# Two graph attention layers on one core: the products for the last layer's vectors, the columns' matmul and a wait of ScalarE are placed anew

## The reference

```python
def gat_layer(x, W, a_s, a_d, b, edge_index, concat):
    h = (x @ W).reshape(n, H, C)
    alpha_s = jnp.einsum('nhc,hc->nh', h, a_s)
    alpha_d = jnp.einsum('nhc,hc->nh', h, a_d)
    e = jax.nn.leaky_relu(alpha_s[src] + alpha_d[dst], NEG_SLOPE)
    m = jax.ops.segment_max(e, dst, num_segments=n)
    e = jnp.exp(e - m[dst])
    denom = jax.ops.segment_sum(e, dst, num_segments=n)
    alpha = e / (denom[dst] + EPS)
    out = jax.ops.segment_sum(h[src] * alpha[:, :, None], dst, num_segments=n)
    return out.reshape(n, H * C) + b
h = jax.nn.elu(gat_layer(x, W1, a_src1, a_dst1, b1, edges, concat=True))
out = layernorm(x + gat_layer(h, W2, a_src2, a_dst2, b2, edges, concat=True))
```

## Time and profile before

| | us |
|---|---|
| median of 3 runs (643.67 to 646.6) | 646.37 |
| the profiled execution, its own time | 646.89 |
| its span (first to last instruction) | 645.1 |
| PE busy (98%) | 631.8 |
| VectorE busy (83%) | 538.0 |
| ScalarE busy (52%) | 337.5 |
| POOL busy (32%) | 209.5 |
| mean granted TensorE clock | 0.999 |

### The profile page before, as it was taken

The page is one execution under the profiler, slowest core; times in us unless marked ns, Lnnn a source line. Parts: engine busy times, 40 slices in busy tenths (PEclk is TensorE's granted clock), DMA queues, the critical chain, the costliest instruction groups (busy, mean ns, idle before and its releaser), DMA issues.

```text
span 645.1 us, 9269 instructions
## 1 busy us (share of the span) xinstructions
PE 631.8 (98%) x3378; PEld 538.6 (83%) x3378; DVE 538.0 (83%) x960; ACT 337.5 (52%) x570; POOL 209.5 (32%) x133
## 2 busy tenths in 40 slices
PE   9999999999999999999999999989999899999996
PEld 5766568989888898989898989978898789887885
DVE  8999997889979877768676968797789868898976
ACT  7899982536534744553444535253544444533382
POOL 2000000140643824085406740474116540351230
PEclk9999999999999999999999999999999999999999
DMA  9322502125144323051304320450215230500002
GB/s 323 152 75 75 167 6 99 49 60 186 53 144 161 110 99 98 1 186 59 99 1 130 115 75 0 144 175 24 74 47 199 74 99 0 196 26 0 1 2 98
DMA packets 22172, 59.34 MB, mean 92 GB/s; under 512 B 2544, under 2 KB 2800, under 8 KB 22128
## 3 DMA queue, kind: packets, MB, share of 16 engines
q1 hardware_dynamic: 21984, 58.69, 27.6%
q10 hardware_dynamic: 144, 0.07, 0.0%
HBM read 54.03 MB, written 4.72 MB: 91 GB/s over the span
## 4 chain that ended last, share of the span: by engine, by line
PE 82%; DVE 13%; issue 3%; ACT 2%; DMA 0%; DVEq 0%; ACTq 0%
PE O L1378 22%; PE R L1268 9%; PE R L1274 9%; PE R L1271 9%; PE O L1285 7%; PE R L1345 6%; PE R L1351 6%; PE R L1348 6%; DVE L L875 2%; DVE ohd L726 1%; DVE junk L785 1%; DVE junk L766 1%; DVE L L869 1%; DVE y L880 1%; PE O L1345 1%
## 5 line engine op out<-in xcount | busy, mean ns | idle before, releaser
L1182 POOL TENSOR_TENSOR W2l<-Wr,W2h 128x768 fp32r<-128x768 f32 x48 | 91.9, 1936 | 129.2 <-ACT W2h L440 129.2
L1268 PE MATMUL R<-W1h,xTh 128*128 128x384 f32 x312 | 106.7, 342 | 1.8 <-DVE L L869 1.2
L1271 PE MATMUL R<-W1l,xTh 128*128 128x384 f32 x312 | 105.3, 338 | 2.9 <-POOL W1l L1176 2.9
L1274 PE MATMUL R<-W1h,xTl 128*128 128x384 f32 x312 | 105.0, 337 | 0.0
L1186 POOL TENSOR_TENSOR Pl<-L,Ph 128x512 fp32r<-128x512 f32 x34 | 55.2, 1644 | 153.1 <-ACT Ph L491 153.1
L1176 POOL TENSOR_TENSOR W1l<-Wr,W1h 128x768 fp32r<-128x768 f32 x30 | 59.2, 1986 | 130.1 <-ACT W1h L429 129.8
L766 DVE CUSTOM_DVE_ANT_0 junk<-h,abc 128x768 bf16<-128x768 f32 x64 | 67.0, 1047 | 25.6 <-ACT h L452 24.3
L1378 PE MATMUL O<-W2h,gh 128*128 128x256 f32 (+1 forms) x384 | 78.5, 339 | 0.0
L1378 PE MATMUL O<-W2h,gl 128*128 128x256 f32 (+1 forms) x384 | 77.5, 336 | 0.0
L1378 PE MATMUL O<-W2l,gh 128*128 128x256 f32 (+1 forms) x384 | 77.2, 335 | 0.0
L1345 PE MATMUL R<-Ph,hh 128*128 128x512 f32 x168 | 66.2, 394 | 0.0
(11 more groups left out here) (203 smaller groups left out, 1184.2 us busy)
## 6 DMA issues: line engine op xcount, KB each, us to landing
Wr<-in_W SPq DMA_DIRECT2D x101, 384.0 KB, 3.7
abc<-in_as SPq DMA_DIRECT2D x9, 384.0 KB, 5.0
abc<-in_ad SPq DMA_DIRECT2D x9, 384.0 KB, 5.5
h_rows<-h SPq DMA_DIRECT2D x8, 384.0 KB, 2.3
hl<-h_rows SPq DMA_DIRECT2D x8, 384.0 KB, 5.4
xin<-in_xT SPq DMA_DIRECT2D x6, 256.0 KB, 5.8
xr<-in_x SPq DMA_DIRECT2D x1, 1536.0 KB, 6.8
out<-res SPq DMA_DIRECT2D x4, 384.0 KB, 2.3
```

The source lines that it names most:

```text
L1182: e.tensor_tensor(W2l[:, m % N2, :], Wr[:, n, :], W2h[:, m % N2, :].bitcast(f32), ALU.subtract).then_inc(s_w2l, 1)
L1268: e.matmul(bank[:, 0:HALF], xTh[:, f, xs], hi[:, ws], start=f == 0, stop=False)
L1271: e.matmul(bank[:, 0:HALF], xTh[:, f, xs], lo[:, ws], start=False, stop=False)
L1274: m = e.matmul(bank[:, 0:HALF], xTl[:, f, xs], hi[:, ws], start=False, stop=f == FT - 1)
```

## The change

- `V_ROWS` and `V_SCORES`: W2 block 1 moves from the place behind the terms of head 5 to the place behind row tile 2 of head 6, and block 4 from behind the terms of head 6 to behind row tile 2 of head 7. Behind the terms of heads 5 and 6 one block each is left (0 and 3), ahead of `rows`. The loads move in SyncE's queue with them.
- `columns` of heads 3 to 6 moves into C block 2, ahead of its last group of eight matmuls.
- ScalarE waits for rm (`s_r12`) before it casts W2 block 5, in heads 3 to 7.
- adm moves from the terms to ahead of the maxima.
- `sources(2)` in head 1's turn stands behind C block 4, before behind block 3.
- In the last stage hl of row tile 0 is made ahead of the fourth row 875, and `tail_denominators` stands behind the first row block's products of the last tile t, before ahead of them.

```diff
@@ -27,3 +27,3 @@
 
-    V_ROWS, V_SCORES = {H - 2: (2,), H - 1: (5,)}, {H - 3: (0, 1), H - 2: (3, 4)}
+    V_ROWS, V_SCORES = {H - 2: (1, 2), H - 1: (4, 5)}, {H - 3: (0,), H - 2: (3,)}
 
@@ -619,2 +619,4 @@
                     high_w2(h - 1, 4)
+
+                    e.wait_ge(s_r12, 2 * h + 2)
                     high_w2(h - 1, 5)
@@ -792,4 +794,15 @@
 
+            by_tile = quad[:, :].unsqueeze(1).broadcast_to([128, NT, 4])
+
+            def by_quarter(a):
+                return a.unsqueeze(2).broadcast_to([128, NT, 4])
+
             def maxima(h, lo, hi, bank):
 
+                if h:
+
+                    if h == 1:
+                        e.wait_ge(s_four, 11)
+                    e.wait_ge(s_asd, 8 * h + 8 if h < H else 8 * H + 1)
+                    e.tensor_tensor(adm[:, :, :], by_quarter(asd[:, h % 2, 1, :]), by_tile, ALU.mult).then_inc(s_adm, 1)
                 for t in range(lo, hi):
@@ -816,9 +829,2 @@
                 n = 2 * h if h < H else 2 * H + lo
-                turned = h > 0
-                by_t, by_b = quad[:, :].unsqueeze(1).broadcast_to([128, NT, 4]), (lambda a: a.unsqueeze(2).broadcast_to([128, NT, 4]))
-                if turned:
-
-                    if h == 1:
-                        e.wait_ge(s_four, 11)
-                    e.tensor_tensor(adm[:, :, :], by_b(ad), by_t, ALU.mult).then_inc(s_adm, 1)
                 e.wait_ge(s_amx, NT * h + hi)
@@ -826,4 +832,4 @@
                 e.wait_ge(s_zm, n // 2 + 1)
-                if turned:
-                    e.tensor_tensor(zmm[:, :, :], by_b(zm[:, :]), by_t, ALU.mult).then_inc(s_zmm, 1)
+                if h:
+                    e.tensor_tensor(zmm[:, :, :], by_quarter(zm[:, :]), by_tile, ALU.mult).then_inc(s_zmm, 1)
                     e.wait_ge(s_zmm, h)
@@ -858,5 +864,7 @@
 
-            def scores(h, n, lo, hi, b1k):
+            def scores(h, n, lo, hi, b1k, between=None):
                 d0, d1 = 128 * lo, 128 * hi
                 for u in range(NT + 1):
+                    if between and u == NT:
+                        between()
                     if u < NT:
@@ -1037,4 +1045,4 @@
                         if t == 2:
-                            for k in V_ROWS.get(h, ()):
-                                products_W2(k, 8 * h + 6)
+                            for i, k in enumerate(V_ROWS.get(h, ())):
+                                products_W2(k, 0 if i else 8 * h + 6)
                     maxima(h, 0, NT, ring_bank("as", h, 0))
@@ -1044,7 +1052,4 @@
                     for i, k in enumerate(V_SCORES.get(h, ())):
-                        if i == 1:
-                            rows(h)
                         products_W2(k, 0 if i else 8 * h + 8)
-                    if h not in V_SCORES:
-                        rows(h)
+                    rows(h)
                     scores(h, h, 0, NT, ring_bank("r1", h, 0))
@@ -1105,6 +1110,8 @@
             rows(H)
-            scores(H, H, 0, NT, ring_bank("r1", H, 0))
-            for t in range(NT):
+            def low_h2(t):
                 e.wait_ge(s_hh, NT * H + t + 1)
                 e.tensor_tensor(hl[:, t, :], res[:, t, :], hh[:, t, :].bitcast(f32), ALU.subtract).then_inc(s_hl8, 1)
+            scores(H, H, 0, NT, ring_bank("r1", H, 0), lambda: low_h2(0))
+            for t in range(1, NT):
+                low_h2(t)
             e.wait_ge(s_P, NT * H + NT)
@@ -1461,5 +1468,9 @@
                             half_B(h + 1, n // 2, n % 2, take("B", h + 1, n))
-                    stage_C(h - 1, c, between=(lambda h=h: denominators(h)) if c == FT - 1 else None,
-                            at=1 if h == H - 1 else 2)
-                    if c == 3 and h == 1:
+                    between = at = None
+                    if c == FT - 1:
+                        between, at = (lambda h=h: denominators(h)), 1 if h == H - 1 else 2
+                    if c == 2 and EARLY <= h < H - 1:
+                        between, at = (lambda h=h: columns(h, take("x", h, 0))), 2
+                    stage_C(h - 1, c, between=between, at=at)
+                    if c == 4 and h == 1:
                         sources(2, 24)
@@ -1467,3 +1478,3 @@
                         sources(h, 8 * h + 8)
-                    if h > 1 and c == (0 if h == 2 else 1 if h == H - 1 else 2):
+                    if (h, c) in ((2, 0), (H - 1, 1)):
                         columns(h, take("x", h, 0))
@@ -1541,4 +1552,2 @@
             for t in range(NT):
-                if t == NT - 1:
-                    tail_denominators()
                 for d in range(2):
@@ -1546,2 +1555,4 @@
                         stage_D(d, t, i)
+                    if t == NT - 1 and d == 0:
+                        tail_denominators()
             for d in (2, 3):
```

## The result

| | before | after |
|---|---|---|
| median, us | 645.64 (4 runs, 643.67 to 646.6) | 638.03 (4 runs, 637.97 to 638.21) |
| profiled execution, its span | 646.89, 645.1 | 638.01, 636.2 |
| head 5, head 6 | 71.4, 71.0 | 67.70, 67.94 |
| PE busy, share | 631.8, 98% | 628.5, 99% |

The ratio is 0.9886, with a 95% interval of 0.9861 to 0.9912: 7.6 us faster, where 638.0 was forecast. The runs after lie within 0.24 us of each other, those before within 2.9.

What follows compares the result with a forecast made beforehand. PE, busy 98% of the span, was taken as the bound, stalling in heads 5 and 6 on late VectorE work. Terms 3.7 + 3.1 + 0.7 + 0.9 = 8.4 us off 646.89 gave 638.5, lowered to 638.0; range 636.3 to 641.6.

Steps and rivals of the forecast that it cites:

- Products, head 5, 3.7: Head 5: moving product 1 off VectorE's path between terms and scores removes PE's whole stall, 3.7 us.
- Products, head 6, 3.1 of 3.30: Head 6: moving product 4 to head 7 wins 3.1 us; 0.2 of the 3.30 stays, through later casts, loads and evictions.
- Columns, 0: Heads 3 to 6: columns' matmul 1.38 us earlier, PE not waiting; worth 0, but puts head 5 ahead.
- adm, 0: Terms: adm leaves VectorE's chain for idle time, r12 comes 0.1 to 0.2 us earlier; worth 0 by itself.
- ScalarE's wait, 0: Before W2 block 5: the later cast and W2l cost 0; up to 1.0 us a head if the cover were gone.
- rival C: Heads 3 to 6: r12 delayed beyond 1.55 us, PE stands at the columns; slower, 653.4 us; chance 0.04.
- sources(2), 0.7: Head 1: one C block later, PE no longer waits for VectorE's sums; 0.7 us, or 0 if lost again at the maxima.
- Tail, 0.9: Last stage: hl of tile 0 first removes PE's 0.96 us loss, and the denominators' later place preserves it; 0.9 us.
- the toss-up: Last stage: POOL's third Pl or VectorE's L875 may go first, making the tail's gain 0.4 or 0.9 us.
- Rival A: Head 6: pinned Wr slots and late transfers, or POOL's W1l, keep its 3.1 us stall; 641.1 us; chance 0.12.
- B: Heads 5 and 6: POOL makes VectorE late, so most of the 7.0 us stays; 644.8 us; chance 0.07.
- the signs of being wrong: Head 4 beyond 67.7 us, PE waiting at the columns on rm, or a new PE wait for sources in heads 6 or 7.

Runs made afterwards that it cites:

- run 9: Kernel after, with W2 block 3 moved from behind rm in head 6 to head 7: 638.77 us.
- Run 3: Kernel after, with the columns' matmul of heads 3 to 6 back behind C block 2: 638.22 us.
- run 6: Kernel after, with adm's multiplication back among the head's terms, behind the maxima: 638.43 us.
- run 7: Kernel after, with the last stage's hl of row tile 0 back behind the fourth row: 639.31 us.
- run 8: Kernel after, with the last layer's denominators back ahead of the fourth row tile's products: 639.20 us.
- run 10: Kernel after, with sources(2) back behind C block 3 of head 1: 639.19 us.
- run 2: Kernel after, with the old product tables and the old places of rows: 641.28 us, ratio 0.9931 against the kernel before.
- run 5: Kernel before, with only ScalarE's wait for rm added ahead of the cast of W2 block 5: 645.44 us, ratio 0.9998.
- run 12: Kernel after, with the old product tables and the columns behind C block 2, ScalarE's wait kept: 644.56 us, ratio 0.9967 against the kernel before.
- run 4: Kernel after, without ScalarE's wait for rm: 638.81 us.
- run 1: Kernel before, with only the products' two tables changed and rows behind the one product left: 640.26 us, ratio 0.9902.
- run 11: Kernel after, with the old product tables and without ScalarE's wait for rm: 643.07 us, ratio 0.9951 against the kernel before.

## Why the prediction was right

The time was 638.03 where 638.0 was forecast. Step by step:

- **Products, head 5, 3.7.** 3.73 came. The transposes start 13.47 us into the head, 0.25 behind head 4's, inside the 1.4 ahead to 0.3 behind; it was the late case, with the second pass on W2l.
- **Products, head 6, 3.1 of 3.30.** 3.05 came, and 0.24 stayed. The fourth sum ends 23.89 us in, 0.79 behind head 4's (0.5 to 0.8 was said). The 0.24 are slips between matmuls where PE reuses a bank after ScalarE's copy of h, at 499.97 and 503.36, which is the eviction named. In run 9, with product 3 gone from head 6, they are gone too. How much stays differs a little from profile to profile: 67.92 to 68.19 in runs 3, 6, 7, 8 and 10. One size was off: the sums of row tile 3 start 0.9 later, not 0.6, and are still in time.
- **Columns, 0.** Run 3 agrees, with the new tables. With the old ones and the wait they had a value, since they let the transposes start (run 2 against 5 and 12). The prediction had this in one clause ("it is what puts head 5 ahead above") but no price; head 5 did not come out ahead.
- **adm, 0.** The time agrees (run 6), the reason does not. I wrote that r12 would come 0.1 to 0.2 earlier. It ends 9.94 us into head 5 in both kernels: adm had run in a gap in which zm had to wait for the last maximum's accumulator anyway. Nor did zm give its place to zmm in head 5: it met the W2l as before (1.87).
- **ScalarE's wait, 0.** It costs nothing, as said: no wait of PE on W2l or W1l. But it also wins 0.3 to 0.6 us in head 6 (run 4), which had no term in the sum. Without it the columns' new place hurts, by rival C's mechanism. The sum holds all the same, since its 3.1 for head 6 assumed PE on time at the columns, which the wait secures. The step that fell short is the list of what the wait does.
- **sources(2), 0.7.** 0.76, and 0.83 when undone (run 10). Nothing took it back.
- **Tail, 0.9.** 1.07, the whole rest behind head 6. The race of the toss-up was won: VectorE's product with the counts began at 611.88, POOL's Pl at 612.10. The argument that the denominators must move by what hl gains was right and needed (runs 7 and 8).
- **The sum.** 8.4 were forecast against the profiled execution and 8.9 came, 0.3 of it start-up. From that to the median I took 0.5 off. That step was a guess of the wrong kind: the spread before goes with the stall, since the tables alone bring the runs within 0.5 (run 1). On medians the change is 7.6, where 8.4 were forecast. The two slips cancel, so the mechanism and the terms are borne out, but that the total agrees to 0.03 is luck.

Rival A fell with head 6's 67.94, B with run 1, and C needed 1.55 us of delay, which the kernel after does not have. None of the signs of being wrong came: head 4 is 67.70, and heads 3 to 7 have no wait on rm or at the sources. The products before row tile 3 are passes of 0.95 to 0.96 in heads 6 and 7, as was said.

## What to carry to other kernels

Work that has to share SBUF with another engine's stream is priced by its place: the same pass took 0.96 us in a gap and 2.65 beside POOL. So fill the gaps in which the other engine is idle before touching the code itself. When two edits only pay together (hl and the denominators, the wait and the columns), undoing one looks as if it carried the whole gain. Test the pair and both singles before giving either a price. And a kernel whose runs scatter may be telling of a race for a resource: here the spread went from 2.9 us to 0.24 with the change.

## What I had not expected of the hardware

After PE had stood for 1.46 and 0.59 us in head 5, the granted clock fell to 0.50 for the next stretch of 4 us and 0.74 in the one after (run 2), at a price of 1.9 us. In run 12 it fell likewise in head 6, behind 1.45 and 0.59, but not in head 5, behind 1.46 and 0.59. The kernel before and run 11, with stands of the same lengths, kept their full clock there in their profiled executions. What decides it no run here shows. And an element count says little under contention: zm, of 128x4 elements, took 1.87 us in head 5 and 0.94 in head 6 of the same execution, each time until an instruction of POOL's ended.
